# An audio tower with a routed expert stage on one core: the expert of a block taken from its row number, a smaller blank fill, new instruction orders, one filler piece

## The reference

```python
# 1. token stage, per sequence
h = silu(conv1d(xt, w_compress)); h = silu(conv1d(h, w_main, padding=1)); h = conv1d(h, w_expand)
y = layer_norm(h + x); ff = gelu(y @ w_ff1 + b) @ w_ff2 + b; y = layer_norm(ff + y)
h = sliding maximum of y over 3 tokens                      # 373 tokens are left
# 2. attention with a normalized input n = layernorm(h)
h = h + softmax((n Wq + bq)(n Wk + bk)^T / sqrt(128)) @ n
# 3. mixture of 8 experts, the best 2 for each token, n = layernorm(h)
gate = softmax(relu(n @ gw1 + gb1) @ gw2 + gb2); the 2 largest, softmaxed again, are the weights
h = h + sum over the 2 of weight * (gelu(n @ we1[e] + be1[e]) @ we2[e] + be2[e])
```

## Time and profile before

| | us |
|---|---|
| median of 3 runs | 252.01 |
| lowest and highest | 250.09, 252.61 |
| the profiled execution | 250.11 |
| its span, first to last instruction | 248.4 |

### The profile page before, as it was taken

One profiled execution on the slowest core, in us unless ns is written; L12 is line 12 of the kernel. 1 busy time (PEld: TensorE's weight loads), 2 busy tenths in 40 slices (PEclk: granted clock), 3 DMA queues, 4 the chain that ended last, 5 costly groups with the idle time before them and its releaser, 6 DMA issues.

```text
span 248.4 us, 5630 instructions
## 1 busy us (share of the span) xinstructions
PE 220.9 (89%) x1621; PEld 176.2 (71%) x1621; DVE 159.1 (64%) x694; ACT 136.3 (55%) x303; POOL 125.9 (51%) x200
## 2 busy tenths in 40 slices
PE   7898999999999989989999887999799759989990
PEld 7565888778478646958569855888588459778780
DVE  0279699999997989898858463752322313215795
ACT  2235894977695769538982157644544323454510
POOL 8466556636303788888888416372633252643000
PEclk9999999999999999999999999999999997999998
DMA  5999999940100220112111255454536465620773
GB/s 132 248 250 298 352 393 390 393 162 0 31 3 1 52 55 22 44 44 73 45 47 45 55 170 198 144 174 153 203 120 254 148 215 192 223 70 13 206 220 91
DMA packets 28449, 36.81 MB, mean 148 GB/s; under 512 B 5387, under 2 KB 20036, under 8 KB 28419
## 3 DMA queue, kind: packets, MB, share of 16 engines
q1 hardware_dynamic: 24289, 32.25, 40.5%
q0 software_dynamic: 3680, 4.04, 6.0%
q10 hardware_dynamic: 450, 0.16, 0.3%
HBM read 10.61 MB, written 15.79 MB: 106 GB/s over the span
## 4 chain that ended last, share of the span: by engine, by line
POOL 21%; PE 20%; DVE 17%; SPq 14%; issue 12%; DMA 11%; ACT 3%; DVEq 0%; POOLq 0%; ACTq 0%
POOL xs L543 14%; DMA blk_x<-xs 5%; SPq L444 4%; POOL rstd L519 4%; SPq L443 3%; DVE stat L689 3%; PE PS L1206 3%; SPq L434 3%; DMA xt_sb<-in_xt 3%; PE PS L1197 3%; PE PS L1174 2%; SPq L433 2%; DVE x_sb L923 2%; DVE acc L960 2%; PE PS L1117 2%
## 5 line engine op out<-in xcount | busy, mean ns | idle before, releaser
L548 POOL DMA_INDIRECT ys<-yblk,blk_x x37 | 36.1, 975 | 46.7 <-DVE yblk L951 40.7
L543 POOL DMA_INDIRECT xs<-rows_x,pos_x x30 | 36.5, 1218 | 9.3 <-issue 9.0
L1174 PE MATMUL PS<-xt_sb,w_all 128*128 128x373 f32 x96 | 36.9, 485 | 1.2 <-ACT xt_sb L641 1.0
L1181 PEld LDWEIGHTS PS<-w_all,gd 128*125 128x125 f32 x288 | 34.4, 190 | 3.9 <-ACT gd L661 1.1
L1181 PE MATMUL PS<-w_all,gd 128*125 128x128 f32 x288 | 35.9, 276 | 0.5 <-ACT gd L661 0.4
L661 ACT ACTIVATE gd<-PS,bias 128x373 f32<-128x373 f32 x48 | 26.9, 573 | 17.1 <-PE PS L1174 14.4
L672 ACT ACTIVATE gb_t<-PS,blk_w 128x128 f32<-128x128 f32 x58 | 17.8, 366 | 28.0 <-PE PS L1206 20.4
L519 POOL TENSOR_TENSOR rstd<-ve,mhalf 125x3 f32<-125x3 f32 x32 | 27.9, 872 | 2.5
L516 POOL TENSOR_TENSOR ve<-mv,eps 125x3 f32<-125x3 f32 x32 | 6.4, 199 | 34.8 <-DVE mv L693 34.4
L951 DVE TENSOR_TENSOR yblk<-PS,blk_w 128x128 f32<-128x128 f32 x29 | 8.1, 286 | 24.4 <-PE PS L1206 22.6
L923 DVE SCALAR_TENSOR_TENSOR x_sb<-PS,comb,x_sb 125x128 f32<-125x128 f32 x72 | 20.7, 343 | 4.6 <-PE PS L1181 4.0
(11 more groups left out here) (201 smaller groups left out, 444.1 us busy)
## 6 DMA issues: line engine op xcount, KB each, us to landing
xs<-blank SPq DMA_DIRECT2D x1, 9675.0 KB, 29.7
blk_w<-w_all SPq DMA_DIRECT2D x29, 321.0 KB, 2.5
blk_x<-xs SPq DMA_DIRECT2D x37, 64.5 KB, 1.9
...
```

Of the source, the lines that this page charges most:

```text
L543: pool.indirect_dma_start(xs, bass.IndirectOffsetOnAxis(ap=pos_x[:, b // 2, s, i:i + 1], axis=0), rows_x[:, k, s, j, :], None).then_inc(s_ ...
L548: pool.indirect_dma_start(ys, bass.IndirectOffsetOnAxis(ap=blk_x[n % SLOTS][:, t, D:XW].bitcast(u32), axis=0), yblk[n % YBUF][:, t, :], No ...
L1174: pe.matmul(f[:, 0:TP], w_all[:, k % E, c * 128:(c + 1) * 128], x32[:, DENSE[k // E], 0:TP], start=True, stop=True).then_inc(S["D1"], 1)
L1181: last = pe.matmul(f[0:P, j * D:(j + 1) * D], gd[:, n % GD, c, OFF[j]:OFF[j] + P], w_all[:, n % E, H + c * D:H + (c + 1) * D], start=(c == ...
```

## The change

SP no longer reads `tab_e`: the expert of a block is the row register of its `lx` divided by `CAP`, which becomes 2048. `tab_e` and the DVE instruction that made it are gone; an instruction that caps `tab_x` at the last block of the table is new. Blocks beyond the last used one now read the last block of expert 7, which no token can reach, so the table has 8 * 2048 = 16384 rows. All five orders are new. Only w.0 is left of the filler, ahead of a1.0, with 5 matmuls. The loads of x and xt are issued in another order.

```diff
-CAP = -(-T * NS // BLK) * BLK
-SPARE = E * CAP
-ROWS_X = SPARE + BLK * (1 + NDYN)
-KMAX = CAP // BLK - 1
+MOST = -(-T * NS // BLK)
+CAP = 2048
+assert MOST < CAP // BLK
+ROWS_X = E * CAP
+KMAX = MOST - 1
...
-w.0:0 a1.0:0 w.1:1 a2.0:0 a2.1:1 ft.0:2 a1.1:3 a3.0:1 a3.1:0 cb.0:4 a2.2:2 a2.3:3 w.2:5 a1.2:1 a1.3:5 bf.0:1
...
+w.0:0 a1.0:0 a2.0:0 a2.1:1 cb.0:0 a3.0:1 a3.1:2 a1.1:0 bf.0:1 a2.2:0 a2.3:3 a1.2:2 a4.0:0 a3.2:3 a3.3:4 a4.1:2
...
-WARM = (11, 6, 6, 6, 4, 2, 2, 4, 2, 3)
+WARM = (5, 3, 4, 5, 1, 5, 2, 3, 1)
...
             sp.dma_start(rows6[:], b_rows[:, 0:6 * D].rearrange("o (r d) -> (o r) d", d=D)).then_inc(S["rows6"], 16)
-            load_x(sp, 1)
             sp.dma_start(wf1_p[:], wf1).then_inc(S["wmid"], 16)
             for s in range(2):
                 sp.dma_start(wf2_p[HALF[s], s, :], wf2).then_inc(S["wmid"], 16)
-            load_xt(2)
-            load_xt(3)
+            load_x(sp, 1)
             for q in range(2, Q):
+                load_xt(q)
                 load_x(sp, q)
...
+                    row_of_block[n] = row
...
-                    e = sp.value_load(tab_e[0:1, k:k + 1], min_val=0, max_val=E - 1)
-                    sp.dma_start(blk_w[k % WSLOTS][:], w_all[:, bass.ds(e, 1), :].rearrange("p o d -> p (o d)"))\
+                    sp.dma_start(blk_w[k % WSLOTS][:], w_all[:, bass.ds(row_of_block[n] // CAP, 1), :].rearrange("p o d -> p (o d)"))\
                         .then_inc(s_bw[k % WSLOTS], 16)
...
-                    dve.tensor_scalar(tab_e[:], eb[:], float(E - 1), None, ALU.min)
...
-                    dve.scalar_tensor_tensor(tab_x[:], block_no[0:1, :], float(BLK), adj[:],
-                                             ALU.mult, ALU.add).then_inc(S["tab"], 1)
+                    link(dve.scalar_tensor_tensor(adj[:], block_no[0:1, :], float(BLK), adj[:], ALU.mult, ALU.add))
+                    dve.tensor_scalar(tab_x[:], adj[:], float(ROWS_X - BLK), None, ALU.min).then_inc(S["tab"], 1)
```

More of the change, by code:

```diff
@@ L68 @@
[L68 to L72, removed]
@@ new lines @@
+a2.4:1 a2.5:5 a5.0:2 ft.0:3 a1.3:0 a6.0:2 a6.1:4 a3.4:5 a3.5:1 a2.6:3 a2.7:0 a4.2:6 fn.0:7 a7.0:2 a4.3:3 a7.1:4
+a3.6:0 a3.7:5 a5.1:3 hr.0:4 hr.1:2 a6.2:3 a6.3:2 a4.4:7 b1.0:1 bq.0:1 b1.1:7 sc0.0:1 sc1.0:0 bq.1:7 sc2.0:4
+a4.5:3 a7.2:6 sc0.1:7 sc1.1:1 pt0.0:4 pt1.0:2 pt2.0:6 a7.3:0 sc2.1:4 at.0:6 a5.2:3 pt0.1:4 hr.2:1 pt1.1:7
+pt2.1:0 a6.4:3 at.1:1 a6.5:0 b1.2:7 a4.6:6 hr.3:4 a4.7:2 bq.2:7 h1.0:1 a5.3:2 sc0.2:7 sc1.2:4 a7.4:3 sc2.2:2
+b1.3:6 a6.6:5 bq.3:3 pt0.2:2 pt1.2:1 h1.1:4 a7.5:0 sc0.3:2 pt2.2:3 sc1.3:4 sc2.3:6 at.2:1 g1.0:0 hr.4:2 a7.6:5
@@ new lines @@
+L2.15:2 D1.24:4 L2.16:1 T.19:2 L1.17:0 D2.10:7 ct.2:0 L1.18:2 T.20:3 L2.17:5 T.21:6 L1.19:0 L2.18:3 T.22:5
+L1.20:2 D1.25:0 L2.19:6 L1.21:2 D2.11:3 T.23:7 L2.20:2 D1.26:0 T.24:6 L1.22:5 D1.27:4 L2.21:1 T.25:0 L1.23:3
+T.26:7 L2.22:1 L1.24:6 D1.28:0 D2.12:1 L1.25:6 L2.23:7 T.27:3 T.28:4 L2.24:5 D1.29:7 L1.26:0 D1.30:1 T.29:7
+L2.25:5 T.30:3 L1.27:4 L2.26:0 L1.28:5 T.31:6 D1.31:4 L2.27:0 L1.29:1 L1.30:5 T.32:0 L2.28:4 D1.32:1 D2.13:3
+L2.29:6 T.33:4 L1.31:7 L1.32:5 L2.30:0 T.34:4 L2.31:7 L1.33:6 T.35:5 D1.33:0 L2.32:1 D1.34:6 L1.34:7 D1.35:5
@@ L97 @@
-xT.26 yv.21 xT.27 xT.28 yv.22 yv.23 yv.24 da.12 xT.29 yv.25 yv.26 xT.30 da.13 yv.27 xT.31 xT.32 yv.28 yv.29
-yv.30 yv.31 da.14 yv.32 yv.33 xT.36 yv.34 yv.35 bd.2 yv.36 da.15 da.16 da.17 da.18 fin.0 fin.1 fin.2 da.19 da.20
-fin.3 da.21 da.22 da.23 fin.4
+cb.0 a3.0 a3.1 l1.0 l1.1 bf.0 a3.2 a3.3 ft.0 a6.0 a6.1 l2.0 l2.1 a3.4 mp.0 a3.5 hr.0 fn.0 hr.1 l3.0 a6.2 a3.6
+l1.5 a6.3 sc0.0 sc1.0 bq.1 sc2.0 l2.3 a3.7 sc0.1 be1.0 sc1.1 sc2.1 mp.1 at.0 hv.2 hr.2 a6.4 l3.2 at.1 hv.3 hr.3
+a6.5 sc0.2 l3.3 sc1.2 sc2.2 a7.4 h1.0 l4.1 pt0.2 a6.6 sc0.3 pt1.2 sc1.3 mp.2 sc2.3 at.2 g2.0 hr.4 g3.0 at.3 a6.7
@@ L100 @@
+yv.24 yv.25 yv.26 yv.27 yv.28 xT.31 xT.33 yv.29 yv.30 xT.34 yv.31 yv.32 xT.35 yv.33 xT.36 yv.34 da.13 yv.35
+yv.36 bd.2 da.14 da.15 da.16 da.17 fin.0 da.18 fin.1 fin.2 da.19 da.20 fin.3 da.21 fin.4 da.22 da.23
 """
 ACT_ORDER = """
-a1.0 a2.0 a2.1 a1.1 a1.2 a2.2 a2.3 a4.0 a4.1 a5.0 a2.4 a2.5 l1.3 a1.3 a4.2 l2.0 a2.6 a4.3 a7.0 a7.1 a2.7 a5.1
-l1.5 hv.1 a4.4 a4.5 b1.0 bq.0 a5.2 l2.2 sc0.0 sc1.0 sc2.0 l2.3 pt1.0 pt2.0 a7.3 pt0.0 l1.6 sc0.1 l2.4 sc1.1
-sc2.1 pt0.1 pt1.1 pt2.1 a7.4 l4.0 h1.0 b1.2 l2.5 bq.2 l1.7 a7.5 h1.1 b1.3 g1.0 bq.3 sc0.2 a4.7 sc1.2 sc2.2 g2.0
@@ L123 @@
 SP_ORDER = """
-c4.1 c4.2 c4.3 c4.5 c4.4 lx.0 lx.1 lx.2 lw.8 lw.9 lx.3 lx.4 lx.5 lx.6 lw.10 lx.7 lw.11 lx.8 lw.12 lx.9 lx.10
-lw.13 lx.11 lx.12 lw.14 lx.13 lx.14 lw.15 lx.15 lw.16 lx.16 lw.17 lx.17 lx.18 lw.18 lx.19 lx.20 lx.21 lw.19
-lw.20 lx.22 lx.23 lw.21 lx.24 lx.25 lw.22 lw.23 lw.24 lw.25 lx.26 lw.26 lx.27 lx.28 lx.29 lw.27 lw.28 lw.29
-lx.30 lw.30 lx.31 lw.31 lx.32 lw.32 lx.33 lw.33 lw.34 lx.34 lx.35 lw.35 lw.36 lx.36 od.0 yl.0 yl.1 yl.2 out.0
-yl.3 out.1 yl.4 out.2 od.1 out.3 od.2 out.4
+c4.1 c4.2 c4.3 c4.4 c4.5 lx.0 lx.1 lx.2 lx.3 lx.4 lx.5 lx.6 lx.7 lx.8 lw.8 lx.9 lw.9 lx.10 lw.10 lx.11 lw.11
+lx.12 lx.13 lw.12 lx.14 lw.13 lw.14 lx.15 lx.16 lw.15 lx.17 lw.16 lx.18 lw.17 lx.19 lx.20 lw.18 lw.19 lw.20
+lx.21 lx.22 lw.21 lw.22 lx.23 lx.24 lw.23 lx.25 lw.24 lw.25 lx.26 lx.27 lx.28 lw.26 lw.27 lw.28 lx.29 lx.30
+lw.29 lx.31 lw.30 lx.32 lw.31 lx.33 lw.32 lx.34 lw.33 lx.35 lw.34 od.0 lx.36 lw.35 lw.36 yl.0 yl.1 yl.2 yl.3
+out.0 od.1 out.1 yl.4 out.2 out.3 out.4 od.2
 """
@@ L417, in _ @@
                 .then_inc(s_blank, 16)
+            row_of_block = {}
             for name, n in pieces(SP_ORDER):
```

71 lines of the change are left out of this document (33 added, 38 removed).

## The result

| | before | changed |
|---|---|---|
| median of 4 runs each, us | 251.49 | 241.0 |
| lowest and highest, us | 250.09, 252.61 | 240.56, 241.27 |
| span of the profiled execution, us | 248.4 | 239.5 |

The ratio is 0.958, 95% interval 0.953 to 0.964. The changed kernel is faster by 4.2%, 10.5 us. The forecast was 239.0 us. In the groups of experiments a few executions came out over 1.5% longer than the fastest one of their kernel; the ratios and the medians given there leave them out.

The account below looks back on a forecast made before the run. SP was taken to bound the stretch of the blocks, PE next. Span 248.4 - 1.0 - 11.9 + 1.1 = 236.6 us, forecast 239 us; own range 235.5 to 243, 8 in 10 from 234 to 247.5.

Parts of the forecast that it names:

- Part 1: From first T to last yv: expert taken from the row register, 82.1 to 70.2 us, with waits for rows -7.3.
- The clock: Term of the stretch of the blocks: PE work lost at the lower granted clock comes back, -1.7 us.
- The moved work: Term of the stretch of the blocks: two D2 and one transpose of h1 leave it, -2.9 us.
- the slots' or the passage through ACT: Reasons for PE waits in the blocks returning: 7 weight slots, or a block's one-by-one passage through PE and ACT.
- Part 2: From last yv to the end of the span: one more da behind the first fin, +1.1 us.
- Part 3: Front and scatters up to the first T: scatters begin later, but the first T comes 1.0 us earlier.
- the three norms moved ahead of the scatters: On POOL, three norm pieces placed ahead of the scatters save 3 x 1.4 = 4.2 us between them.
- The filler, taken as nothing: In the front: 41 fewer filler matmuls on PE count as nothing, at most -3 or +4 us, since DVE sets the pace.
- Part 4: Blank fill of 16384 rows and new load order: nothing, with at most 1.5 us to lose.
- The later front: Rival: more DVE work and late norms delay the scatters; first T 7 us later, 246 us; chance 0.18.
- SP's waits: Rival: freed SP does not free PE in the blocks, about 5 us of waits return, 244 us; chance 0.12.
- The lower clock: Rival: with filler gone, PE's clock stays at 1.2 GHz through the token stage, 258 us; chance 0.07.

Follow-up runs that it names:

- the SP part alone: Changed kernel with the kernel before's PE, DVE, ACT and POOL orders, filler and load order; 249.79 us, ratio 0.976 to the kernel before.
- the register reads put back: Changed kernel with SP again reading `tab_e` for each of 29 weight copies, and DVE writing it; 260.19 us, ratio 1.017 to the kernel before.
- the rows written in: Changed kernel with the rows of the 29 later blocks as constants, so SP reads no table; 235.97 us, ratio 0.939 to the kernel before.
- group 2: Second group of experiments, on the front; its base is the changed kernel unaltered, 246.15 us, ratio 0.957 to the kernel before.
- The kernel with filler in the front: Changed kernel with eight filler pieces in its front instead of one; 249.81 us, ratio 0.978 to the kernel before.
- my seam: Join in the changed kernel given the kernel before's front up to the first T, putting h1.7 ahead of T.0; 250.86 us, ratio 0.977.

## Why the prediction was right, and where it was off

**What bounds the kernel.** SP's queue bounded the blocks, as read from the earlier trace rows. Shown by the SP part alone (0.976 and 0.6 us of waits for rows, with PE's order untouched), by the register reads put back (1.017), and by the rows written in (0.939).

**Part 1, the stretch of the blocks: -11.9 forecast, -12.5 measured.** Term by term: PE's idle time fell by 7.1 us (forecast -7.3), its waits for rows alone by 5.6. The clock gave 1.8 us: 506 instructions took 70.7 us before and 68.9 at full clock in the SP run (forecast -1.7). The moved work gave the rest of PE's busy time, 68.9 - 65.3 = 3.6 us (forecast -2.9). What failed is the sentence that SP stops being the bound. I compared SP's 58.6 us with PE's 70.2 over the whole stretch. But late in it SP issued one pair directly behind the other, at 1.79 us, and that is no less than the 64.3 / 37 = 1.74 us in which PE can do a block with what stands beside it. The 3.7 us of waits that stayed were SP's, not the slots' or the passage through ACT that I had named for them; the run without table reads shows it, since slots and passage are the same there and no wait is left. In group 2 the same kernel's PE waited only 0.5 us for rows, and idled 5.5 us for the most part behind ACT and DVE; there the passage did count, beside the "remote" waits of those two.

**Part 2, the end: +1.1 forecast, +0.5 measured.** The kernel with SP alone changed has the old order of the end and took 23.9 us from the last yv. So the new end costs nothing that these runs tell apart, and the added da was hidden where DVE waited for PE:

```profile
222.26 0.87 DVE L923 SCALAR_TENSOR_TENSOR x_sb<-PS,comb,x_sb 125x128 f32<-125x128 f32 x3 [1.08 <-PE PS L1180]
223.04 0.87 DVE L959 SCALAR_TENSOR_TENSOR acc<-yg,w_top,x_sb 125x128 f32<-125x128 f32 x3
```

The first fin stands 7.0 us behind the last yv, as before (6.9), with that da just ahead of it.

**Part 3, the front: -1.0 forecast, +3.1 measured.** This is the mis-sized term, and it is the whole error: +4.1 here, -0.6 and -0.6 in the other two, make 2.9 us of span. What set the first T was DVE's rank for the pair 4/5: I had it 1.3 us earlier, and it came 3.5 us later, as did that pair's first scatter (124.3 for 120.8); the last scatter and the first T then followed by 3.4 and 3.1 us. So the step that failed is the count of DVE's work and waits ahead of that rank. It has two pieces, and beside them stands a wrong reason.

DVE from its first addition (L729) to the rank that starts the scatters (L888), before and changed:

```profile
13.53:82.22 68.69, 65.42 (x557) 50.92 (x556) 61.26 (x265) 49.17 (x101) 33.93 (x74) 1.00 0.61 200
```

```profile
13.67:87.35 73.68, 68.64 (x534) 49.85 (x535) 66.03 (x288) 57.24 (x116) 37.98 (x84) 0.98 0.52 171
```

This is the first piece. DVE's busy time grew by 4.8 us; its idle time hardly did, 7.4 and 7.7. I had counted +3.5. The 1.3 us that I missed are as large as the five short instructions of ft.0 (L777 to L781, 1.3 us), which before ran at 10.9 us, while DVE waited for the first data anyway, and now stands behind the first additions, at 24.7. I had counted pieces between two points, not whether they stood in a gap.

The second piece is larger. From there to the rank of the pair 4/5 the time is 37.26 before and 35.66 changed, with DVE busy 33.5 and 30.1: idle time grew from 3.7 to 5.6 us. Its waits there:

```profile
DVE nmax L822 <- PE PS L1098: 1.2, 1, 1.2
DVE gsum L853 <- ACT ge L649: 0.9, 1, 0.9
DVE lg L843 <- PE PS L1137: 0.6, 1, 0.6
```

By my two counts this part should have been 4.8 us shorter (-1.3 less +3.5); it was 1.6. I had given the lesser work there 4.8 us, where it was 3.5, and no new wait, where 1.9 us came.

The wrong reason is that of the three norms moved ahead of the scatters: I took them for 4.2 us of POOL's time. POOL's row did get shorter, from 53.15 to 50.91 us, 2.2 us only, since POOL then waited 1.2 and 1.4 us for the ranks of the pairs 2/3 and 4/5. And what they are there for is another thing: ACT's new order needs them early, at a price of 3.3 us for p3.5 and 8.9 for p2.7 if they come late. I had named this hold as a danger for the scatters (they would wait for the norms), and never looked at the other side, who waits for a norm behind a scatter.

**The filler, taken as nothing.** Not contradicted for the new order: more of it gained nothing in either run. In the old order it was worth 2.6%, so my reason, that DVE sets the pace and the filler stands where PE would wait, fails there. The two orders give it different worths, so it has to be priced together with the order that it stands in.

**Part 4, fill and load order, nothing:** right within the measurement.

**The rivals.** The later front came true for its sign and half its size (3.1 us in place of 7 to 8). SP's waits came back in part, 3.7 us; of the reasons given for it, slots and passage were not the cause, but the third was, that SP needs about as long for a block as PE. The lower clock came, for the first 21 us and again from 34 to 38 and from 92 to 96 us, where the mean granted clock was 0.57 both times, so for nearly 28 us in all. Half that length would be 14 us, and the span lost nothing like it: the whole front came 3.1 us late. The kernel with the rows written in has the same front, and there the second a2 already ran at full speed (1.21 us; the third took 1.55); its first scatter still came at 90.0 us, against 89.9. That the time hid behind DVE is argued from this, not shown.

**What stays open.** The price of the old front ahead of the new blocks, since my seam spoiled that run. Why the kernel with filler in the front is 3.7 us slower than its base; the two traces differ by 2.7 us (first T 1.9, stretch 0.2, end 0.6). What the "remote" waits are. And a version that keeps the table but beats the changed kernel: `tab_x` is ready at 133.66 us and SP makes its first load of a block at 143.99, so there are 10 us in which SP could read rows into registers. That wasn't tried; the run with the rows written in, which leaves out the register work too, suggests that its gain is at most some 5 us.
